# A perceiver block on one core: the first chunk's keys and values projected in the first stage, the queries last

## The chip, the core and the metric

The kernel runs on one core of a Trainium2 chip. Its engines work through their own instruction lists and wait for each other on semaphores: TensorE (PE, matmuls and transposes, with weight loads listed as PEld), VectorE (DVE), ScalarE (ACT), GpSimd (POOL), and SyncE (SP), which issues the DMAs. The metric is the device time of one execution in microseconds (us), lower is better.

## What is computed

Three layers, each added to its input: cross attention of 8 x 128 tokens over a context of 8 x 2048 rows, a differential self attention, and a mixture of eight experts. The change touches the first one alone:

```python
q = (layernorm(x) @ wq.T + bq)      # x: 8 batches x 128 tokens x 512
k = (ctx @ wk.T + bk)               # ctx: 8 batches x 2048 rows x 512
v = (ctx @ wv.T + bv)
scores = einsum('bhqd,bhkd->bhqk', q, k) / sqrt(32)    # 16 heads of 32
x = x + (softmax(scores) @ v) @ wo.T + bo
```

## The kernel before

Every product of a projection is computed as three fp32r matmuls, high x high, high x low and low x high (`product`, L41 to L45), since an operand is split in two parts: ACT copies the transposed operand out of a PSUM bank as its high part, and DVE subtracts that from the bank to get the low part. So every operand goes through a *transpose unit* on PE (four 128x128 transposes into one bank), one ACT copy and one DVE split. A *product unit* is 12 matmuls of 128x512 (four blocks of the contraction, three matmuls each) into one bank.

The program is a row of blocks with a barrier between them. The first is `queries_and_weights`. One list, `order`, is the sequence of units on PE, and the loops of ACT and DVE walk the same list: the four transpose units of wq (kind "w", 2), eight of the normalized x (kind "x"), then eight query products (kind "q", group g and half of the tokens), each followed by one transpose unit of wk or wv. Four PSUM banks are used in turn. SP loads x in two transfers, then the query bias, wq, wk, wv and the first chunk of the context; a query group is written to HBM (`q_d`) when both of its halves are out. DVE computes the layer norm of x (`Norm`: statistics, then small steps of which the square root is ACT's), writes the normalized x, and evicts the query products with their bias.

The second block is `cross_attention`. The context goes through it in 32 chunks of 512 rows, four per batch. Time is counted in beats, with eight beats for a chunk. In each beat PE's list holds at most one step of each kind: `transposed(beat)` gives the chunk and the transpose unit ("T"), every second beat; `projected(beat)` the key ("K", four) or value ("V", four) product of the chunk; from beat 20 on the scores, and from beat 32 the outputs. The loop runs from `FIRST` = -8, so that beats -8 to -1 hold the transposes of chunk 0 and beats 0 to 7 the products of chunk 0 and the transposes of chunk 1. Beat 8 begins with the first transpose unit of chunk 2. Three banks (`b_work`) are used in turn. SP loads two pieces of 256 rows per chunk into `cin`, each when its piece of the chunk before is transposed.

Output projection, self attention and the experts follow in blocks of their own, which the change does not touch.

Of the kernel before, what the change touches and what calls it, by code (L numbers as in the profile page):

```python
# [16 lines left out]
B = 8  # L17
# [48 lines left out]
class Shared:  # L66


    def __init__(self, nc, ctx):
# [18 lines left out]
        self.x_sb = at(0, "x_sb", B, D)  # L88
        self.w_sb = [at(QUARTER + i * KD * D, f"w_sb{i}", KD, D) for i in range(3)]
# [17 lines left out]
        self.q_out = [sem(f"q_out{i}") for i in range(2)]  # L107
# [10 lines left out]
class Norm:  # L118
# [20 lines left out]

    def tile_stats(self, x, t):  # L140

        self.nc.vector.bn_stats(self.stats[:, t, :], x[:, t, :]).then_inc(self.step, 1)
# [45 lines left out]
def queries_and_weights(nc, x, ctx_in, w, q_d, cin, shared):  # L188

    with ExitStack() as ctx:
# [3 lines left out]
        def sem(name):  # L197
            return ctx.enter_context(nc.semaphore(name))

        ident, x_sb, w_sb, wkT, wvT = shared.ident, shared.x_sb, shared.w_sb, shared.wkT, shared.wvT  # L200
        xn = sb("a_xn", [P, B, D])
        bq = sb("a_bq", [P, KD])
        wqT = [sb(f"a_wqT{i}", [P, KD, D], F32R) for i in range(2)]
        xT = [sb(f"a_xT{i}", [P, KD, TOK], F32R) for i in range(2)]
        q_st = sb("a_q", [P, 2, TOK])
        bank = [ctx.enter_context(nc.psum_tensor(f"a_ps{i}", [P, 512], F32)) for i in range(4)]
# [6 lines left out]
        hi_done = sem("a_hi")  # L213
        lo_done = sem("a_lo")
        normed = sem("a_normed")
        q_out = shared.q_out
# [5 lines left out]
        SPLIT = {u: i for i, u in enumerate(u for u in order if u[0] != "q")}  # L222
        RING = len(bank)
        block = ctx.enter_context(nc.Block())

        @block.sync
        def _(sp):
            for i in range(2):
                part = slice(i * (B // 2), (i + 1) * (B // 2))
                sp.dma_start(x_sb[:, part, :], x[part].rearrange("b p d -> p b d")).then_inc(x_in[i], 16)  # L230
            with nc.allow_non_contiguous_dma(reason="512 numbers"):
                sp.dma_start(bq[:, :], w["bq"].rearrange("(g p) -> p g", p=P)).then_inc(b_in, 16)
            for i in (2, 0, 1):
                sp.dma_start(w_sb[i], weights[i][0].rearrange("(o p) d -> p o d", p=P)).then_inc(w_in[i], 16)
            for c in range(2):
                sp.dma_start(cin[:, c, :, :], ctx_in[0, c * 2 * P:(c + 1) * 2 * P, :]
                             .rearrange("(o p) d -> p o d", p=P)).then_inc(shared.cin_in[c], 16)
            for g in range(G):
                sp.wait_ge(lo_done, place["q", g, 1] + 1)
                sp.dma_start(q_d[g].rearrange("b p t -> p b t"),  # L240
                             q_st[:, g % 2, :].rearrange("p (b t) -> p b t", b=B)).then_inc(q_out[g % 2], 16)
# [6 lines left out]
        def _(pe):  # L248
            pe.wait_ge(const, 2)
            for u, (kind, i, j) in enumerate(order):  # L250
                if u >= RING:
                    pe.wait_ge(lo_done, u - RING + 1)
                out = bank[u % RING]
                if kind == "w":
                    if j == 0:
                        pe.wait_ge(w_in[i], 16)
                    for o in range(KD):
                        last = nc.tensor.transpose(out[:, o * P:(o + 1) * P], w_sb[i][:, o, j * P:(j + 1) * P],
                                                   ident[:, :])
                elif kind == "x":  # L260
                    if j == 0:
                        pe.wait_ge(normed, 4 * i + 4)
                    for t in range(4):
                        last = nc.tensor.transpose(out[:, t * P:(t + 1) * P], xn[:, 4 * i + t, j * P:(j + 1) * P],
                                                   ident[:, :])
                else:
                    if (i, j) == (0, 0):

                        pe.wait_ge(lo_done, u)
                    for k in range(KD):  # L270
                        last = product(nc, out[:, :], [a[:, k, i * P:(i + 1) * P] for a in wqT],
                                       [a[:, k, j * 512:(j + 1) * 512] for a in xT], k == 0, k == KD - 1)
                last.then_inc(full, 1)

        def to(u):

            kind, i, j = u
            if kind == "w":
                return [a[:, j, :] for a in weights[i][1]]
            return [a[:, j, i * 512:(i + 1) * 512] for a in xT]  # L280

        @block.scalar
        def _(act):
            norm.scalar(act)
            for unit in SPLIT:
                act.wait_ge(full, place[unit] + 1)
                nc.scalar.activation(to(unit)[0], bank[place[unit] % RING][:, :], ACT.Copy).then_inc(hi_done, 1)

        @block.vector
        def _(dve):  # L290
            for t in range(B):
                if t % 4 == 0:
                    dve.wait_ge(x_in[t // 4], 16)
                norm.tile_stats(x_sb, t)
            norm.vector(dve)
            norm.done(dve)
            for t in range(4):
                norm.apply(x_sb[:, t, :], xn[:, t, :], t).then_inc(normed, 1)
            dve.wait_ge(b_in, 16)
# [1432 lines left out]
```

## Time and profile before

| | us |
|---|---|
| median of 3 runs | 1833.36 |
| lowest and highest | 1832.06, 1834.14 |
| the profiled execution | 1831.57 |
| its span | 1829.8 |
| PE busy in it | 1710.6 (93%) |
| DVE busy | 1200.3 (66%) |
| ACT busy | 962.1 (53%) |
| POOL busy | 695.6 (38%) |

The rows come from the profiled execution. Its span runs from the first instruction to the last; the 1.8 us beside it lie around the program. A matmul's busy time overlaps the next one's, so the distance from start to start is what a matmul or a unit costs. An idle time before a group is followed by what released it, as `<-DMA x_sb`.

### The profile page before, as it was taken

The numbers are of one execution on the slowest core, as the hardware profiler recorded it, in microseconds if no ns is written. First come the engines' busy times: TensorE is split into PE (matmuls) and PEld (weight loads), VectorE is DVE, ScalarE is ACT, GpSimd is POOL, SyncE is SP. The second block draws the span as 40 slices with busy tenths as digits, with TensorE's granted clock in tenths as the row PEclk, the third lists the DMA queues.
The fourth block names the chain that finished last, engine by engine and source line by source line (L and its number), as shares of the span: only waits on it lengthen the run. The fifth ranks groups of instructions, "written<-read, shape, count | busy, mean of one in ns | idle before, by whom it ended". The sixth has DMA issues, their size and how long they took to land. (4 is left out here: it accounts for less than half of the span.)

```text
span 1829.8 us, 37829 instructions
## 1 busy us (share of the span) xinstructions
PE 1710.6 (93%) x15768; PEld 1376.8 (75%) x15768; DVE 1200.3 (66%) x1631; ACT 962.1 (53%) x1470; POOL 695.6 (38%) x315
## 2 busy tenths in 40 slices
PE   6899999999999999999999998567999689979999
PEld 5688888888888888888888887566887466658886
DVE  5126887878778778778778787767323677753223
ACT  2236666666666666666666666653210678730000
POOL 0003555555555555555555554002001466622220
PEclk9999999999999999999999999789999899999999
DMA  4211111111011011011110101042560533101101
GB/s 162 73 47 38 32 35 41 27 39 41 27 39 42 27 39 42 28 39 37 32 39 30 39 16 63 16 132 109 179 184 2 161 91 103 58 25 46 49 19 46
DMA packets 104192, 105.00 MB, mean 57 GB/s; under 512 B 7263, under 2 KB 72799, under 8 KB 104044
## 3 DMA queue, kind: packets, MB, share of 16 engines
q1 hardware_dynamic: 104044, 102.83, 18.5%
q8 instruction: 117, 1.92, 0.4%
q14 instruction: 31, 0.25, 0.0%
HBM read 79.74 MB, written 23.07 MB: 56 GB/s over the span
## 5 line engine op out<-in xcount | busy, mean ns | idle before, releaser
L528 POOL TENSOR_TENSOR b_acc<-b_acc,b_s 128x1024 f32<-128x1024 f32 x168 | 458.6, 2730 | 268.5 <-ACT b_s L731 258.1
L793 DVE TENSOR_TENSOR b_mx<-b_psS,b_mx 128x512 f32<-128x512 f32 x480 | 331.3, 690 | 50.0 <-PE b_psS L600 36.9
L760 DVE TENSOR_TENSOR b_s<-b_s,b_mb 128x2048 f32<-128x2048 f32 x128 | 350.9, 2743 | 15.7 <-ACT b_mb L718 15.7
L731 ACT ACTIVATE b_s<-b_s 128x2048 f32<-128x2048 f32 x128 | 245.1, 1915 | 67.1 <-DVE b_s L760 67.1
L740 ACT ACTIVATE b_s<-b_psS 128x2048 f32<-128x2048 f32 x128 | 241.1, 1883 | 56.3 <-DVE b_mx L793 55.9
L43 PE MATMUL b_work<-cT,wkT 128*128 128x512 f32 x512 | 210.7, 412 | 0.0
L43 PE MATMUL b_work<-wvT,cT 128*128 128x512 f32 x512 | 209.4, 409 | 0.0
L44 PE MATMUL b_work<-cT,wkT 128*128 128x512 f32 x512 | 200.8, 392 | 0.0
L45 PE MATMUL b_work<-cT,wkT 128*128 128x512 f32 x512 | 200.5, 392 | 0.0
L45 PE MATMUL b_work<-wvT,cT 128*128 128x512 f32 x512 | 200.2, 391 | 0.0
L44 PE MATMUL b_work<-wvT,cT 128*128 128x512 f32 x512 | 200.0, 391 | 0.0
L523 POOL TENSOR_TENSOR b_acc<-b_s 128x1024 f32<-128x1024 f32 x28 | 66.9, 2389 | 281.2 <-PE b_psO L637 171.0
L690 ACT ACTIVATE b_kT<-b_work,b_bk 128x512 f32<-128x512 f32 x128 | 88.1, 688 | 157.3 <-PE b_work L45 154.8
L600 PE MATMUL b_psS<-b_q,b_kT 32*128 32x128 f32 x4096 | 152.0, 285 | 16.1 <-ACT b_s L740 16.1
L600 PEld LDWEIGHTS b_psS<-b_q,b_kT 32*128 32x128 f32 x4096 | 127.6, 188 | 41.4 <-issue 41.2
L614 PE MATMUL b_psO<-b_s,v_sb 128*32 128x128 f32 x4096 | 143.5, 282 | 6.1 <-DVE b_oq L773 4.3
L783 DVE TENSOR_TENSOR cT<-b_work,cT 128x512 fp32r<-128x512 f32 x128 | 87.4, 684 | 83.9 <-ACT cT L723 83.9
L614 PEld LDWEIGHTS b_psO<-b_s,v_sb 128*32 128x32 f32 x4096 | 108.4, 112 | 33.7 <-issue 33.2
L1679 DVE SCALAR_TENSOR_TENSOR x<-f_ps,f_gate,x 128x512 f32<-128x512 f32 x64 | 47.9, 751 | 119.7 <-PE f_ps L45 119.2
L43 PEld LDWEIGHTS b_work<-cT,wkT 128*128 128x128 f32 x512 | 96.6, 189 | 30.1 <-issue 5.6
L43 PEld LDWEIGHTS b_work<-wvT,cT 128*128 128x128 f32 x512 | 96.1, 188 | 24.5
L45 PEld LDWEIGHTS b_work<-cT,wkT 128*128 128x128 f32 x512 | 96.6, 189 | 21.4
(224 smaller groups left out, 3056.7 us busy)
## 6 DMA issues: line engine op xcount, KB each, us to landing
cin<-in_ctx SPq DMA_DIRECT2D x64, 512.0 KB, 3.7
q_scratch<-d_st SPq DMA_DIRECT2D x32, 256.0 KB, 2.5
k_scratch<-d_st SPq DMA_DIRECT2D x32, 256.0 KB, 2.5
e_q<-q_scratch SPq DMA_DIRECT2D x16, 512.0 KB, 3.5
k_sb<-k_scratch SPq DMA_DIRECT2D x64, 128.0 KB, 3.7
experts_sb<-in_L_ffn_expert_w SPq DMA_DIRECT2D x8, 1024.0 KB, 5.3
x_sb<-in_x SPq DMA_DIRECT2D x2, 1024.0 KB, 7.0
q_scratch<-a_q SPq DMA_DIRECT2D x4, 512.0 KB, 3.2
```

Of the source, the lines that this page charges most:

```text
L43: nc.tensor.matmul(out, lhs[0], rhs[0], start=first, stop=False)
L44: nc.tensor.matmul(out, lhs[0], rhs[1], start=False, stop=False)
L45: return nc.tensor.matmul(out, lhs[1], rhs[0], start=False, stop=last)
L528: nc.gpsimd.tensor_tensor(acc[:, :, :], acc[:, :, :], s[:, buf, 2 * i:2 * i + 2, :], ALU.add).then_inc(sum_done, 1)
L600: last = nc.tensor.matmul(psS[:, j, t * P:(t + 1) * P], kT[h, at + t * P:at + (t + 1) * P], q[h, m % 3, :], start=True, stop=True)
L614: last = nc.tensor.matmul(psO[j * HD:(j + 1) * HD, 0:P], v[:, at + j * HD:at + (j + 1) * HD], s[:, n % BUFS, i, j * P:(j + 1) * P], start= ...
L690: nc.scalar.activation(kT[:, at:at + 512], bank[:, :], ACT.Identity, bias=bk[:, u:u + 1]).then_inc(k_done, 1)
L731: nc.scalar.activation(part, part, ACT.Exp, scale=SCALE).then_inc(exp_done, 1)
L740: nc.scalar.activation(s[:, n % BUFS, :, :].rearrange("p t (j q) -> p t j q", j=HG), psS[:, :, :].rearrange("p j (t q) -> p t j q", t=CHUN ...
L760: nc.vector.tensor_tensor(s[:, n % BUFS, :, :], s[:, n % BUFS, :, :], mb[:, :].rearrange("p (o n) -> p o n", o=1).broadcast_to([P, CHUNK, ...
L783: nc.vector.tensor_tensor(context_place(cT[1], p, n), two(work[BANK["T", p, n]]), f32(context_place(cT[0], p, n)), ALU.subtract).then_inc( ...
L793: nc.vector.tensor_tensor(mx[:, :, :], part, mx[:, :, :], ALU.max).then_inc(mx_done, 1)
```

## The change

The first block is rewritten as `queries_and_first_chunk`. It now also transposes chunks 0 and 1 of the context and computes the four key and four value products of chunk 0. The order is: wk, chunk 0, then key and value products with the transposes of wv, chunk 1 and wq between them, then x and the queries, first half of the tokens first. It has eight banks. SP issues wk, the two pieces of chunk 0, wv, both biases, x in four transfers, wq, then the reloads of `cin`. x is placed in free columns of the key buffer `kT` and normalized there in place. ACT evicts keys, values and queries, and waits for both biases before its first instruction. The queries leave in eight transfers of 256 KB. `cross_attention` starts at beat 8: `FIRST` is 8, its counters of splits, keys and values go on from the first block's. The helpers `key_place`, `context_place` and `two` move out of `cross_attention` unchanged. The core of the diff:

```diff
-        order = ([("w", 2, k) for k in range(KD)] + [("x", half, k) for half in range(2) for k in range(KD)]
-                 + [u for n in range(2 * G) for u in (("q", n // 2, n % 2), ("w", n // KD, n % KD))])
+        order = ([("w", 0, k) for k in range(KD)] + [("c", 0, n) for n in range(4)]
...
+                 + [("x", 0, k) for k in range(KD)]
+                 + [u for g in range(G) for u in (("q", 0, g), ("x", 1, g))] + [("q", 1, g) for g in range(G)])
...
-        bank = [ctx.enter_context(nc.psum_tensor(f"a_ps{i}", [P, 512], F32)) for i in range(4)]
+        bank = [ctx.enter_context(nc.psum_tensor(f"a_ps{i}", [P, 512], F32)) for i in range(8)]
...
+            load_weights(0)
+            for h in range(2):
+                load_context(0, h)
+            load_weights(1)
             with nc.allow_non_contiguous_dma(reason="512 numbers"):
+                sp.dma_start(bk[:, :], w["bk"].rearrange("(g p) -> p g", p=P)).then_inc(b_in, 16)
                 sp.dma_start(bq[:, :], w["bq"].rearrange("(g p) -> p g", p=P)).then_inc(b_in, 16)
...
+                sp.dma_start(parts[:, g, 1:3, :], x[2 * g:2 * g + 2].rearrange("b p d -> p b d")).then_inc(x_in[g // 2], 16)
+            load_weights(2)
+            for p in range(2):
+                for h in range(2):
+                    sp.wait_ge(full, place["c", p, 2 * h + 1] + 1)
+                    load_context(p + 1, h)
...
+                elif kind == "k":
+                    if j == 0:
+                        pe.wait_ge(w_lo, counted("w", 0, KD - 1))
+                        pe.wait_ge(shared.split_done, counted("c", 0, 3))
...
+                    if j == 0:
+                        pe.wait_ge(w_lo, counted("w", 2, KD - 1))
+                        pe.wait_ge(x_lo, counted("x", i, KD - 1))
...
         @block.scalar
         def _(act):
-            norm.scalar(act)
...
+            act.wait_ge(b_in, 32)
+            for u, (kind, i, j) in enumerate(order):
+                if (kind, i, j) == ("c", 1, 2):
+                    norm.scalar(act)
+                act.wait_ge(full, u + 1)
...
+                    nc.scalar.activation(q_st[:, n % 4, :], out[:, :], ACT.Identity,
+                                         bias=bq[:, j:j + 1]).then_inc(q_done, 1)
...
+            for u, (kind, i, j) in enumerate(order):
+                if (kind, i, j) == ("w", 1, 2):
+                    statistics(0)
+                elif (kind, i, j) == ("c", 1, 0):
+                    statistics(1)
+                elif (kind, i, j) == ("c", 1, 2):
+                    norm.vector(dve)
+                    norm.done(dve)
+                elif (kind, i, j) == ("w", 2, 0):
+                    applied(0)
+                elif (kind, i, j) == ("w", 2, 2):
+                    applied(1)
...
-        FIRST, LAST = -SLOT, (SLOTS + 4) * SLOT + 3
+
+        FIRST, LAST = SLOT, (SLOTS + 4) * SLOT + 3
...
-            n = steps(beat, FIRST, 2, SLOTS * CHUNK)
+            n = steps(beat, -SLOT, 2, SLOTS * CHUNK)
...
-                if (x0 := projected(beat - 1)) is not None:
+                if beat > FIRST and (x0 := projected(beat - 1)) is not None:
```

Three places in the engines' lists follow. In them a row is line, instruction, out<-in, shape of the output and the semaphores it waits for.

SP at the start of the first block, before (x, the query bias, the weights, the context):

```order
L230 DMA x_sb<-in_x 128x4x512 x2
L232 DMA a_bq<-in_L_xattn_bq 128x4x1
L234 DMA w_sb_52<-in_L_xattn_wq 128x4x512
L234 DMA w_sb_50<-in_L_xattn_wk 128x4x512
L234 DMA w_sb_51<-in_L_xattn_wv 128x4x512
L236 DMA cin<-in_ctx 128x2x512 x2
L240 DMA q_scratch<-a_q 128x8x128 [waits a_lo] x4
```

and now (`b_kT` is where x is put):

```order
L269 DMA w_sb_49<-in_L_xattn_wk 128x4x512
L265 DMA cin<-in_ctx 128x2x512 x2
L269 DMA w_sb_50<-in_L_xattn_wv 128x4x512
L276 DMA a_bk<-in_L_xattn_bk 128x4x1
L277 DMA a_bq<-in_L_xattn_bq 128x4x1
L279 DMA b_kT<-in_x 128x2x512 x4
L269 DMA w_sb_51<-in_L_xattn_wq 128x4x512
L265 DMA cin<-in_ctx 128x2x512 [waits a_full] x4
L287 DMA q_scratch<-a_q 128x4x128 [waits a_q_done] x8
```

The bias of the queries stood behind x and now stands, with that of the keys, behind wk, two context pieces and wv; x and wq moved to the end.

ACT at the start of the first block, before (`a_full` counts the units that PE has finished):

```order
L180 ACT_TABLE_LOAD
L180 ACTIVATE a_norm_root<-a_norm_veps 128x8 [waits a_norm_step]
L287 ACTIVATE a_wqT<-a_ps 128x512 [waits a_full] x4
L287 ACTIVATE a_xT<-a_ps 128x512 [waits a_full] x8
L287 ACTIVATE wkT_63<-a_ps 128x512 [waits a_full] x4
L287 ACTIVATE wvT_65<-a_ps 128x512 [waits a_full] x4
```

and now (`a_b_in` counts the two bias transfers):

```order
L367 ACT_TABLE_LOAD [waits a_full]
L367 ACTIVATE wkT_62<-a_ps 128x512 [waits a_b_in]
L367 ACTIVATE wkT_62<-a_ps 128x512 [waits a_full] x3
L369 ACTIVATE cT_52<-a_ps 128x2x256 [waits a_full] x4
L374 ACTIVATE b_kT<-a_ps,a_bk 128x512 [waits a_full]
L367 ACTIVATE wvT_64<-a_ps 128x512 [waits a_full] x2
L374 ACTIVATE b_kT<-a_ps,a_bk 128x512 [waits a_full]
L367 ACTIVATE wvT_64<-a_ps 128x512 [waits a_full] x2
L374 ACTIVATE b_kT<-a_ps,a_bk 128x512 [waits a_full]
L369 ACTIVATE cT_52<-a_ps 128x2x256 [waits a_full] x2
```

The square root has moved behind the keys and a value unit, and a wait for the biases stands before the first copy.

PE where the last transpose unit before a query product stands, before (banks are numbered; the transpose unit is one of wk, and its bank is not read by the product behind it):

```order
L45 MATMUL a_ps0<-a_xT0,a_wqT1 128x512
L258 MATMUL a_ps1<-ident,w_sb0_50 128x128 [waits a_w_in0,a_lo]
L258 MATMUL a_ps1<-ident,w_sb0_50 128x128 x3
L43 MATMUL a_ps2<-a_xT0,a_wqT0 128x512 [waits a_lo]
L44 MATMUL a_ps2<-a_xT1,a_wqT0 128x512
```

and now, at the fifth query product (`a_x_lo` counts the splits of x):

```order
L45 MATMUL a_ps6<-a_xT0,a_wqT1 128x512
L334 MATMUL a_ps7<-ident,b_kT 128x128 [waits a_x_lo]
L334 MATMUL a_ps7<-ident,b_kT 128x128 x3
L43 MATMUL a_ps0<-a_xT0,a_wqT0 128x512 [waits a_x_lo,a_w_lo,a_q_done]
L44 MATMUL a_ps0<-a_xT1,a_wqT0 128x512
```

The product at this place now waits for the split of the unit transposed just ahead of it.

## Rows read from the trace of the kernel before

**Rows 1.** Busy by stretch: stretch, us, engines busy (instructions), PE clock, DMA, GB/s.
```profile
0.00:52.48 52.48, 34.20 (x177) 27.85 (x177) 28.99 (x58) 13.40 (x22) 0.81 (x7) 1.00 0.46 153
52.48:85.57 33.09, 28.05 (x128) 23.04 (x129) 5.35 (x8) 8.78 (x15) 0.00 (x0) 0.90 0.31 81
85.57:1200.00 1114.43, 1087.68 (x12493) 883.00 (x12495) 849.96 (x878) 714.97 (x683) 525.50 (x196) 0.99 0.13 37
```

**Rows 2.** Waits of PE, 52 to 1240 us: us in total, times, longest.
```profile
PE b_psS L600 <- ACT b_s L740: 16.1, 7, 5.0
```

**Rows 3.** Timeline of PE, context transposes of beats 2, 8: start, us, instruction.
```profile
67.81 0.60 PE L565 MATMUL b_work<-ident,cin 128*128 128x128 f32 x4
...
85.57 0.60 PE L565 MATMUL b_work<-ident,cin 128*128 128x128 f32 x4
```

**Rows 4.** Timeline of ACT, DVE and PE, 0 to 25 us.
```profile
0.73 1.28 ACT L180 ACT_TABLE_LOAD   x1 [0.73 <-PEq L1721]
6.64 2.47 DVE L142 BATCH_NORM_STATS2 a_norm_stats<-x_sb 128x6 f32<-128x512 f32 x4 [6.64 <-DMA x_sb<-in_x]
9.30 2.47 DVE L142 BATCH_NORM_STATS2 a_norm_stats<-x_sb 128x6 f32<-128x512 f32 x4 [0.19 <-DMA x_sb<-in_x]
...
12.79 0.20 DVE L159 RECIPROCAL a_norm_rstd<-a_norm_root 128x8 f32<-128x8 f32 x1 [0.27 <-ACT a_norm_root L180]
12.85 3.65 PE L258 MATMUL a_ps<-ident,w_sb 128*128 128x128 f32 x16 [12.85 <-DMA w_sb<-in_L_xattn_wq]
13.84 1.92 DVE L184 TENSOR_SCALAR a_xn<-x_sb,a_norm_mv,a_norm_rstd 128x512 f32<-128x512 f32 x4
...
19.89 4.86 DVE L315 TENSOR_TENSOR a_xT<-a_ps,a_xT 128x512 fp32r<-128x512 f32 x8
20.62 2.45 PE L264 MATMUL a_ps<-ident,a_xn 128*128 128x128 f32 x16 [1.77 <-DVE a_xT L315]
24.90 0.47 PE L43 MATMUL a_ps<-a_xT,a_wqT 128*128 128x512 f32 x1 [1.83 <-DVE a_xT L315]
```

**Rows 5.** Timeline of PE, the last unit of the first block.
```profile
50.05 0.60 PE L258 MATMUL a_ps<-ident,w_sb 128*128 128x128 f32 x4
```

**Rows 6.** Timeline of PE, start of the second block.
```profile
52.48 1.52 PE L565 MATMUL b_work<-ident,cin 128*128 128x128 f32 x12 [1.83 <-POOL b_ones L514]
...
56.92 0.66 PE L565 MATMUL b_work<-ident,cin 128*128 128x128 f32 x4 [2.92 <-DVE cT L783]
...
60.43 0.78 PE L43 MATMUL b_work<-cT,wkT 128*128 128x512 f32 x1
```

**Rows 7.** Timeline of PE, ACT and DVE, one round of query product and weight transposes.
```profile
27.74 0.60 PE L258 MATMUL a_ps<-ident,w_sb 128*128 128x128 f32 x4
...
28.38 0.60 ACT L287 ACTIVATE wkT<-a_ps 128x512 fp32r<-128x512 f32 x1 [4.67 <-PE a_ps L258]
...
29.01 0.69 DVE L315 TENSOR_TENSOR wkT<-a_ps,wkT 128x512 fp32r<-128x512 f32 x1 [0.32 <-ACT wkT L287]
...
30.93 0.60 PE L258 MATMUL a_ps<-ident,w_sb 128*128 128x128 f32 x4
```

**Rows 8.** Timeline of SP, the issue of the query bias: start, us of issue.
```profile
1.78 0.51 SPq L232 DMA_DIRECT2D a_bq<-in_L_xattn_bq  x1
```

**Rows 9.** DMA issues, 0 to 130 us: KB each, median us from issue to landing.
```profile
a_bq<-in_L_xattn_bq SPq DMA_DIRECT2D x1, 2.0 KB, 8.2
b_bk<-in_L_xattn_bk SPq DMA_DIRECT2D x1, 2.0 KB, 2.3
```

**Rows 10.** Busy by stretch, two single microseconds: columns as in the first group.
```profile
57.00:58.00 1.00, 0.58 (x4) 0.34 (x4) 1.00 (x2) 0.44 (x2) 0.00 (x0) 0.74 0.83 161
64.00:65.00 1.00, 1.00 (x5) 0.85 (x4) 0.00 (x0) 0.00 (x0) 0.00 (x0) 0.85 0.00 0
```

**Rows 11.** Timeline of ACT, the evictions of key products 0 and 1.
```profile
65.27 0.69 ACT L690 ACTIVATE b_kT<-b_work,b_bk 128x512 f32<-128x512 f32 x1 [3.85 <-PE b_work L45]
68.01 0.69 ACT L690 ACTIVATE b_kT<-b_work,b_bk 128x512 f32<-128x512 f32 x1 [2.06 <-PE b_work L45]
```

More of the change, by code:

```diff
@@ L251, in _ @@
                 if u >= RING:
-                    pe.wait_ge(lo_done, u - RING + 1)
+                    wait_evicted(*order[u - RING])
                 out = bank[u % RING]
@@ L259, in _ @@
                                                    ident[:, :])
+                elif kind == "c":
+                    h, kk = divmod(j, 2)
+                    if kk == 0:
+                        pe.wait_ge(cin_in[h], 16 * (i + 1))
+                    for k in range(2):
+                        for o in range(2):
+                            last = nc.tensor.transpose(out[:, (2 * k + o) * P:(2 * k + o + 1) * P],
+                                                       cin[:, h, o, (2 * kk + k) * P:(2 * kk + k + 1) * P], ident[:, :])
                 elif kind == "x":
@@ L270, in _ @@
                     for k in range(KD):
-                        last = product(nc, out[:, :], [a[:, k, i * P:(i + 1) * P] for a in wqT],
-                                       [a[:, k, j * 512:(j + 1) * 512] for a in xT], k == 0, k == KD - 1)
+                        last = product(nc, out[:, :], [a[:, k, j * P:(j + 1) * P] for a in wqT],
+                                       [a[:, k, i * 512:(i + 1) * 512] for a in xT], k == 0, k == KD - 1)
                 last.then_inc(full, 1)
[L275 to L280, printed above, removed]
@@ L289, in _ @@
         @block.vector
         def _(dve):
[L291 to L299, printed above, removed]
-            for u, unit in enumerate(order):
-                kind, g, half = unit
-                if u == KD:
-                    for t in range(4, B):
-                        norm.apply(x_sb[:, t, :], xn[:, t, :], t).then_inc(normed, 1)
-                if kind == "q":
-                    dve.wait_ge(full, u + 1)
-                    if g >= 2:
-                        dve.wait_ge(q_out[g % 2], 16)
-                    nc.vector.tensor_scalar(q_st[:, g % 2, half * 512:(half + 1) * 512], bank[u % RING][:, :],
-                                            bq[:, g:g + 1], None, ALU.add).then_inc(lo_done, 1)
-                else:
-                    hi, lo = to(unit)
-                    dve.wait_ge(hi_done, SPLIT[unit] + 1)
-                    nc.vector.tensor_tensor(lo, bank[u % RING][:, :], f32(hi), ALU.subtract).then_inc(lo_done, 1)
@@ L318, in cross_attention, with statistics, applied @@
-def cross_attention(nc, x, ctx_in, w, q_d, o_d, cin, shared):
+            def statistics(half):
+                dve.wait_ge(x_in[half], 32)
+                for t in range(4 * half, 4 * half + 4):
+                    norm.stats_of(xs[t], t)
+            def applied(half):
+                for t in range(4 * half, 4 * half + 4):
+                    norm.apply(xs[t], xs[t], t).then_inc(normed, 1)
+            for u, (kind, i, j) in enumerate(order):
[10 more added lines that the diff above has]
+                    applied(1)
+                count = counted(kind, i, j)
+                out = bank[u % RING]
+                if kind == "w":
+                    hi, lo = [a[:, j, :] for a in weights[i][1]]
+                    dve.wait_ge(w_hi, count)
+                    nc.vector.tensor_tensor(lo, out[:, :], f32(hi), ALU.subtract).then_inc(w_lo, 1)
+                elif kind == "c":
+                    hi, lo = [context_place(a, i, j) for a in cT]
+                    dve.wait_ge(shared.hi_done, count)
+                    nc.vector.tensor_tensor(lo, two(out), f32(hi), ALU.subtract).then_inc(shared.split_done, 1)
+                elif kind == "x":
+                    hi, lo = [a[:, j, i * 512:(i + 1) * 512] for a in xT]
+                    dve.wait_ge(x_hi, count)
+                    nc.vector.tensor_tensor(lo, out[:, :], f32(hi), ALU.subtract).then_inc(x_lo, 1)
```

132 lines of the change are left out of this document (88 added, 44 removed), and 3 rows, old and new, of the table order.

## The prediction

> **What bounds the kernel now.** I read the engines' busy times by stretch first. From 85.57 us to 1200 TensorE (PE) is busy 1087.7 of 1114.4 us and no other engine comes near it; from 0 to 52.48 it is busy only 34.2 us, and the next 33.1 us hold 5 us of idling and a granted clock of 0.90 [rows 1]. PE's waits between 52 and 1240 us come next: the largest group there is 16.1 us in seven pieces [rows 2]. So the long middle is a PE conveyor: what enters it earlier should leave it earlier, and the question is the head alone. The mark I use is beat 8 of cross attention, the transposes of chunk 2, which PE starts at 85.57 [rows 3]. From there both kernels run the same list, so the change is worth 85.57 minus the time at which PE reaches that point.
>
> The timeline of the head shows where PE idles: until 12.85 for the queries' weights, then behind norm, transposes and splits until 24.90 [rows 4]. Eight query products and eight weight transposes follow without a gap, to 50.65 [rows 5]. Then the seam between the stages to 52.48, the first chunk's transposes, their splits, and the first key product at 60.43 [rows 6].
>
> **Unit costs.** A transpose unit (four transposes) plus a 12-matmul product takes 30.93 - 27.74 = 3.19 us [rows 7]. A transpose unit plus two products is a third of 85.57 - 67.81 = 17.76, so 5.92 [rows 3]. Hence a product is 2.73 and a transpose unit 0.46 us at full clock.
>
> **What costs nothing.** All units are still done once: 16 products (4 key, 4 value, 8 query) and 28 transpose units before beat 8. The query eviction goes from VectorE (DVE) to ScalarE (ACT), x is normalized in place, x comes in four transfers instead of two, and the queries leave in eight instead of four. ACT then has about 27 us of evictions (28 of 0.6, 16 of 0.6 to 0.7 [rows 7, 11]) beside over 50 us of PE work. The context's reload for chunk 1 stands on SP's queue behind x and the queries' weights: by the pace of term 1 it lands near 24, and PE wants it near 31; if it came later than that, its lateness would be paid. Behind the seam ACT waits again for biases, some 3 us, but PE has then one transpose unit and two products (5.9 us) for the three banks.
>
> **Term 1: when the first key product can start.** It needs eight splits, four of wk and four of context chunk 0. Not PE's transposes end last there but the new first wait of ACT: it stands before every eviction and asks for both bias vectors, which SP issues behind wk, two context pieces and wv, that is behind 3 MB. Before, the two MB of x land at 6.64 and 9.30, 2.66 per MB [rows 4], and the 2 KB bias issued at 1.78 lands 8.2 later, at 9.98 [rows 8, 9]: it went behind the 2 MB and took 0.7 itself. So wv lands at 12.0 and the two biases at 13.4. The eight transpose units (four of them took 3.65 at the start [rows 4]) are done by 12 to 13.5 and fill the eight banks. From 13.4: 0.63 from ACT's first eviction to DVE's first split [rows 7], eight splits in 4.86, 0.15 until PE starts [rows 4]. Key product 0 starts at **19.0**. Bounds: 17.6 if the biases cost nothing of their own, 20.4 if each costs double.
>
> The rows show a bias that waits for what was issued before it. The Trainium skill's page "DMA: Bandwidth & Descriptors", section "Queues, rings and completion order", says that descriptors are taken in ring order, but that completion is not first-in-first-out for the issuing engine. With the first half the term is 19.0, as by the rows; if the second half let these small transfers finish well ahead, it would be that of rival A. The trace agrees with the first half (9.98 behind 9.30) and shows no case of the second.
>
> **Term 2: PE's work from there to the seam.** 16 products are 43.7 us. Eight of the 28 transpose units are done; 20 are left, 9.2 us.
>
> **Term 3: the clock.** PE has then idled for some 6 us. In the trace its granted clock falls to half at about 57.5, after a wait of 2.9 us, 0.7 of work and idling again, and is back at about 64.2 [rows 6, 10]. The key product begun in that state at 60.43 is evicted at 65.27, 4.84 later; the next eviction follows after 2.74 [rows 6, 11]. At full clock it would have been 2.73 + 0.21, so the state costs 1.9. The kernel before pays it after its seam; the changed one pays the same **1.9** at its first key product. Bounds 0 and 4.
>
> **Term 4: two stalls.** The queries' first product follows directly on its four x transpose units: before, the first such unit started at 20.62 and the product at 24.90, 4.28 [rows 4]; less 4 x 0.46 that is **2.4**. And x's last transpose unit stands right before the product that needs it: from start at 27.74 to split done at 29.01 + 0.69, plus 0.15, is 2.11 [rows 7]; less 0.46, plus 0.25 because ACT first evicts a query unit, is **1.9**. Each can be 0.5 off either way. The first has a cover: the norm's root on ACT stands behind value unit 0, evicted near 38.1, and a table load of 1.28 and a root of 0.2 follow; DVE then needs 1.05 for the small steps, 3.84 for eight tiles and 3.65 for six splits [rows 4], to 48.2. It is wanted at 49.7, so 1.5 us are in hand.
>
> **Term 5: the seam.** Before: the last transpose unit starts at 50.05 [rows 5], its split is over 1.96 later [rows 7], at 52.01, and PE starts at 52.48 [rows 6]. After: last product, eviction 0.7, issue of its query transfer 0.5 (the issue in [rows 8]), then 0.47: **1.7**.
>
> **The sum.** 19.0 + 43.7 + 9.2 + 1.9 + 2.4 + 1.9 + 1.7 = 79.8 for beat 8, against 85.57: 5.8 us earlier. The profiled execution took 1831.57 us (its span is 1829.8), so it becomes 1825.8; the three runs have their median at 1833.36, 1.8 higher, and I give the number against that: 1833.36 - 5.8 = **1827.6**. The bounds of the single terms put it between 1825 and 1830.
>
> **Rivals.**
> A. *The biases do not hold ACT.* If they land before the context (behind the seam, on an idle queue, one lands 2.3 us after its issue [rows 9]), ACT starts behind the first transpose unit and a table load, at 8.9; the splits end at 14.4, key product 0 starts at 14.5, and PE has hardly idled, so its clock stays up: 4.5 + 1.9 more, 1821.2. For: their size. Against: the 8.2 us. Chance 0.16.
> B. *Slower: the clock stays at half.* The 1.9 of term 3 came of some four fifths of a product at half clock, so a whole one costs 2.4 more. If the clock came back only after all eight key and value products, that is 19.2 instead of 1.9, and the time is 1845. It is a loss from about 3.2 products at half clock. Against: the same matmuls brought it back within 4 us [rows 6, 10]. Chance 0.05.
> C. *The biases land last.* If the 4-byte packets are served only when all 6.3 MB are in, near 22, key product 0 starts at 27.6 and the time is 1836.2; break-even is a landing at 19.2. Against: the same 8.2 us. Chance 0.06.
> D. *Given back later.* Something behind beat 8 that is tied to time and not to PE's order, such as the clock around the idle pieces near 1200, takes the gain: about 1833. Nothing in the rows ties it so. Chance 0.07.
>
> **How the numbers follow.** The forecast keeps 0.66. About 0.2%, or 3.7 us, is what a measurement of this kernel can tell from no change, so the line lies at 1829.7; of the forecast's 0.66 some 0.06 lie above it. Faster: 0.60 + 0.16 = 0.76. Within: 0.06 + 0.06 (C) + 0.07 (D) = 0.19. Slower: 0.05 (B). The range takes in the forecast's own bounds and rival A, 1820 to 1831; B, C and D are left out.
>
> **What would show it.** ACT's first eviction at about 13.4, released by a bias transfer, and PE idle before key product 0 at 19.0 (A: 14.5; C: 27.6); a granted clock of half for its first 4 us; key and value products then without gaps; a stall of 2.4 before the first query product and of 1.9 before the fifth; chunk 2's transposes at 79.8; from there to the end 1829.8 - 85.57 = 1744.2 as before (D: more). The main step is wrong if ACT's first eviction is not near 13.4, and the premise if that distance changes by more than 2 us.

## The result, and the profile after

| | before | after |
|---|---|---|
| median of 16 runs | 1834.33 us | 1828.93 us |
| lowest and highest | 1829.56, 1839.71 | 1825.63, 1831.22 |
| span of the profiled execution | 1829.8 | 1826.5 |

The ratio is 0.9972, with a 95% interval of 0.9963 to 0.9981: faster by 0.28%, or 5.4 us where 5.8 were forecast, and inside the range of 1820 to 1831. Beat 8 of cross attention, the mark of the prediction, begins at 79.98 us where 79.8 was forecast and 85.57 stood before [rows 3].

Busy time by stretch, after (stretch, us, busy and instructions of PE, PEld, DVE, ACT, POOL, granted clock, DMA share, GB/s), to be read beside [rows 1]; the cuts are beat 8 and the first instruction of the output projection:

```profile
0.00:79.98 79.98, 62.22 (x304) 52.04 (x305) 27.60 (x58) 27.23 (x47) 0.81 (x7) 0.94 0.39 128
79.98:1216.25 1136.27, 1102.37 (x12865) 896.25 (x12865) 863.99 (x888) 725.37 (x689) 525.60 (x196) 0.99 0.13 37
1216.25:1826.50 610.25, 549.86 (x2585) 432.82 (x2600) 300.94 (x677) 215.15 (x743) 168.76 (x112) 0.95 0.28 87
```

The head is 5.6 us shorter with the same PE work before beat 8. The same three stretches of before, cut at the same points of the program, were 85.57, 1136.30 and 607.93 us: the middle kept its length to 0.03 us, and the last third is 2.3 longer. So the profiled execution shows 3.3 of the 5.6 at its end, and the medians show 5.4. What became of the 2.3 is a question of its own, below.

The timeline of SP, PE, ACT and DVE at the start of the changed kernel (start, us, instruction, idle before and what ended it) answers to [rows 4] and [rows 8]:

```profile
2.30 0.77 SPq L269 DMA_DIRECT2D w_sb<-in_L_xattn_wv  x1
3.11 0.65 SPq L276 DMA_DIRECT2D a_bk<-in_L_xattn_bk  x1
3.81 1.72 SPq L277 DMA_DIRECT2D a_bq<-in_L_xattn_bq  x1
...
6.43 3.64 PE L320 MATMUL a_ps<-ident,w_sb 128*128 128x128 f32 x16 [6.43 <-DMA w_sb<-in_L_xattn_wk]
7.60 1.28 ACT L367 ACT_TABLE_LOAD   x1 [7.60 <-PE a_ps L320]
...
9.87 2.42 PE L328 MATMUL a_ps<-ident,cin 128*128 128x128 f32 x16
...
12.58 2.06 ACT L367 ACTIVATE wkT<-a_ps 128x512 fp32r<-128x512 f32 x4 [3.69 <-DMA a_bq<-in_L_xattn_bq]
13.21 2.48 DVE L414 TENSOR_TENSOR wkT<-a_ps,wkT 128x512 fp32r<-128x512 f32 x4 [13.21 <-ACT wkT L367]
...
18.23 0.77 PE L43 MATMUL a_ps<-cT,wkT 128*128 128x512 f32 x1 [5.94 <-DVE cT L418]
```

Every transpose unit that the key products need is over at 12.3. ACT sat idle for 3.69 us until the query bias landed, though the weights it was to copy began to fill the banks at 6.43. PE then idles 5.94 us until the splits are done. Landings, from issue (KB, median us), answer to [rows 9]:

```profile
w_sb<-in_L_xattn_wv SPq DMA_DIRECT2D x1, 1024.0 KB, 9.5
a_bk<-in_L_xattn_bk SPq DMA_DIRECT2D x1, 2.0 KB, 8.8
a_bq<-in_L_xattn_bq SPq DMA_DIRECT2D x1, 2.0 KB, 8.7
```

Added to the issue times: wv lands at 11.8, the key bias at 11.9, the query bias at 12.5.

The two stalls and the seam, timeline of PE, after; the first row is the first half's four x transpose units, behind value product 3:

```profile
46.90 1.91 PE L334 MATMUL a_ps<-ident,b_kT 128*128 128x128 f32 x16
...
50.85 0.47 PE L43 MATMUL a_ps<-a_xT,a_wqT 128*128 128x512 f32 x1 [2.04 <-DVE a_xT L422]
...
55.25 0.61 PE L334 MATMUL a_ps<-ident,b_kT 128*128 128x128 f32 x4
...
67.15 0.47 PE L43 MATMUL a_ps<-a_xT,a_wqT 128*128 128x512 f32 x1 [1.65 <-DVE a_xT L422]
...
79.98 0.65 PE L665 MATMUL b_work<-ident,cin 128*128 128x128 f32 x4 [1.70 <-POOL b_ones L614]
```

And the clock, single microseconds of the changed kernel (columns as above, the granted clock third from the end), as in [rows 10]:

```profile
18.00:19.00 1.00, 0.77 (x2) 0.71 (x3) 0.08 (x1) 0.00 (x0) 0.00 (x0) 0.50 1.04 383
21.00:22.00 1.00, 1.00 (x6) 0.83 (x5) 0.00 (x0) 0.00 (x0) 0.00 (x0) 0.93 1.06 389
...
52.00:53.00 1.00, 1.00 (x4) 0.82 (x3) 0.00 (x0) 0.00 (x0) 0.00 (x0) 0.50 0.08 16
55.00:56.00 1.00, 1.00 (x8) 0.76 (x7) 0.00 (x0) 0.54 (x1) 0.00 (x0) 0.87 0.00 0
```

Half clock stands at 18 us, where the prediction put it. It stands a second time from 52 to 55, behind the stall of 2.04 us, and that was not foreseen: the first query product takes 55.25 - 50.85 = 4.40 until the next unit starts. At full clock it took 2.84 in the kernel before (27.74 - 24.90 [rows 4, 7]).

**The ledger.** PE's idle pieces before beat 8 were, before, 12.85, 1.77 and 1.83 [rows 4], 1.83 and 2.92 [rows 6], and this one, in the timeline of the kernel before:

```profile
59.69 1.09 PE L565 MATMUL b_work<-ident,cin 128*128 128x128 f32 x4 [2.11 <-DMA cin<-in_ctx]
```

That is 23.3 us. After they are 6.43, 5.94, 2.04, 1.65 and 1.70: 17.8. The difference is 5.5. Besides, with four banks each four x transpose units took 2.45 us [rows 4], with eight they take 1.91, about 1.1 in all; and half clock cost some 2.2 before beat 8 in the kernel before and 2.9 in the changed one. Together that is 5.9, against 5.6 at the mark; the 0.3 between them is not explained. PE's busy time before the mark is the same in both profiles, 62.26 and 62.22 us, so the idle pieces carry the gain. The change takes 6.4 off the first wait, since wk is first in the queue where wq stood behind x's 2 MB and the bias, and 5.0 (2.92 and 2.11) off what followed the seam; it gives 5.9 back behind the bias wait.

### The profile page after: what moved, and what is told of

The parts are those of the page before. It is cut to its first block and busy times, and to the rows that moved or that the text cites. A ratio compares the mean times of both kernels' runs of the same rounds, so it can differ in the third digit from the quotient of the medians.

```text
span 1826.5 us, 37824 instructions
## 1 busy us (share of the span) xinstructions
PE 1714.4 (94%) x15753; PEld 1381.1 (76%) x15768; DVE 1192.5 (65%) x1623; ACT 967.7 (53%) x1479; POOL 695.2 (38%) x315
## 3 DMA queue, kind: packets, MB, share of 16 engines
HBM read 79.74 MB, written 23.07 MB: 56 GB/s over the span
## 5 line engine op out<-in xcount | busy, mean ns | idle before, releaser
L43 PE MATMUL b_work<-cT,wkT 128*128 128x512 f32 x496 | 203.5, 410 | 0.0
L43 PE MATMUL b_work<-wvT,cT 128*128 128x512 f32 x496 | 203.0, 409 | 0.0
L45 PE MATMUL b_work<-wvT,cT 128*128 128x512 f32 x496 | 193.9, 391 | 0.0
L44 PE MATMUL b_work<-cT,wkT 128*128 128x512 f32 x496 | 193.8, 391 | 0.0
L44 PE MATMUL b_work<-wvT,cT 128*128 128x512 f32 x496 | 193.8, 391 | 0.0
L45 PE MATMUL b_work<-cT,wkT 128*128 128x512 f32 x496 | 193.6, 390 | 0.0
L875 DVE TENSOR_TENSOR cT<-b_work,cT 128x512 fp32r<-128x512 f32 x120 | 82.0, 684 | 68.7 <-ACT cT L815 68.7
L43 PEld LDWEIGHTS b_work<-cT,wkT 128*128 128x128 f32 x496 | 93.0, 187 | 29.4 <-issue 5.6
L45 PEld LDWEIGHTS b_work<-cT,wkT 128*128 128x128 f32 x496 | 93.1, 188 | 20.6
```

The costliest lines, as they stand in the source:

```text
L43: nc.tensor.matmul(out, lhs[0], rhs[0], start=first, stop=False)
L44: nc.tensor.matmul(out, lhs[0], rhs[1], start=False, stop=False)
L45: return nc.tensor.matmul(out, lhs[1], rhs[0], start=False, stop=last)
L875: nc.vector.tensor_tensor(context_place(cT[1], p, n), two(work[BANK["T", p, n]]), f32(context_place(cT[0], p, n)), ALU.subtract).then_inc( ...
```

## The experiments

All times of beat 8 are those of the first transpose unit of chunk 2 on PE, in the profiled execution of each kernel; ratios are against the kernel before, from runs on the same chip.

### A later bias wait

The wait moves to the first eviction that uses a bias.

```diff
-            act.wait_ge(b_in, 32)
             for u, (kind, i, j) in enumerate(order):
+                if (kind, i, j) == ("k", 0, 0):
+                    act.wait_ge(b_in, 32)
```

> One edit to the changed kernel: ACT's wait for both biases moves from before its first instruction to before the eviction of key product 0, the first that uses one. Theory (the bias wait alone sets the start of the key products, and the idling it causes costs PE its clock): ACT's first eviction at 8.9 instead of 12.58, behind the table load; the last split is then bound by PE's last transpose unit, key product 0 starts at 13.9 instead of 18.23 and runs at full clock, 2.73 instead of 4.17; chunk 2's transposes start 5.7 us earlier, at 74.2, and the time falls by about 5.7 against the changed kernel, near 0.994 of the kernel before. Rival (something else ends just behind the bias wait, such as the context, wv or x by DMA): key product 0 or a unit within the next 20 us waits for a DMA, and less than 3 us are gained.

Timeline of ACT and PE of this kernel:

```profile
7.43 0.60 ACT L368 ACTIVATE wkT<-a_ps 128x512 fp32r<-128x512 f32 x1 [5.42 <-PE a_ps L320]
...
13.59 0.47 PE L43 MATMUL a_ps<-cT,wkT 128*128 128x512 f32 x1 [2.28 <-DVE cT L419]
...
72.47 0.65 PE L666 MATMUL b_work<-ident,cin 128*128 128x128 f32 x4 [1.71 <-POOL b_ones L615]
```

The first key product starts at 13.59 instead of 18.23, and beat 8 comes at 72.47, 7.5 earlier than in the changed kernel. Of these, 4.6 are the start and 1.3 the clock at the first product (2.82 until the next unit instead of 4.17); the remaining 1.6 are the second half-clock phase, which is missing here although the stall before the first query product is as long as before. That part is not the edit's: the phase is missing in a second execution of the unchanged program too, below. The time is 1822.3 us, ratio 0.9939 (0.9918 to 0.9959), which puts it some 6 us below the changed kernel. ACT started even earlier than expected, because its table load now runs at 0.73 and no longer behind PE's first unit. The rival is out: no unit of the next 20 us waited for a DMA. So the wait's place cost the changed kernel 4.6 us of start and at least 1.3 of clock, and that is shown.

### Biases last in the queue

Both bias loads move behind `load_weights(2)`, the wait stays at ACT's head.

> One edit to the changed kernel: SP issues the two biases behind x and the queries' weights instead of ahead of x; ACT's wait stays at its head. Theory: the landing follows the 3 MB now ahead of them, 7.9 us later by the pace of 2.65 us per MB, so ACT's first eviction goes from 12.58 to 20.5, key product 0 from 18.23 to 26.1, and the end by the same 7.9: the time is about 1837, 1.001 to 1.002 of the kernel before, and all of it passes through the long middle. Rival (the middle or the tail takes up a shift of the head): chunk 2's transposes start 7.9 later, but the time grows by less than 5.

```profile
20.99 2.06 ACT L367 ACTIVATE wkT<-a_ps 128x512 fp32r<-128x512 f32 x4 [12.15 <-DMA a_bq<-in_L_xattn_bq]
...
26.64 0.77 PE L43 MATMUL a_ps<-cT,wkT 128*128 128x512 f32 x1 [14.82 <-DVE cT L418]
...
59.67 0.47 PE L43 MATMUL a_ps<-a_xT,a_wqT 128*128 128x512 f32 x1 [2.04 <-DVE a_xT L422]
...
63.66 1.06 PE L334 MATMUL a_ps<-ident,b_kT 128*128 128x128 f32 x4
...
88.81 0.65 PE L665 MATMUL b_work<-ident,cin 128*128 128x128 f32 x4 [1.70 <-POOL b_ones L614]
```

3 MB more ahead of the biases made them 8.4 us later, where 7.9 was expected: from the landing of wv at 12.1 to that of wq at 20.5 the 3 MB took 2.8 us each. The key bias landed at 20.3 and the query bias at 21.0, so the first came 0.3 ahead of wq, which was issued before it. Beat 8 is 8.8 later than in the changed kernel, at 88.81. The time is 1837.6 us, the ratio 1.0013 (1.0001 to 1.0025). By the ratios that is 7.5 us above the changed kernel, with an uncertainty of some 3; the medians, 1837.6 and 1828.9, were not taken side by side. This is the course of rival C, brought about by the order of issue, and the rival of this run, that less than 5 us would arrive at the end, is unlikely. The second half-clock phase is there, behind a stall of 2.04 us again: the first query product takes 63.66 - 59.67 = 3.99.

### Four bias loads instead of two

Each bias is loaded a second time into a tile that nothing reads, and ACT waits for all four.

```diff
+                sp.dma_start(bk2[:, :], w["bk"].rearrange("(g p) -> p g", p=P)).then_inc(b_in, 16)
+                sp.dma_start(bq2[:, :], w["bq"].rearrange("(g p) -> p g", p=P)).then_inc(b_in, 16)
...
-            act.wait_ge(b_in, 32)
+            act.wait_ge(b_in, 64)
```

> One edit to the changed kernel: each bias is loaded twice, the second time into a tile that nothing reads, and ACT waits for all four. It measures what one 2 KB bias transfer in that queue costs. Theory (about 0.7 each, in queue order): ACT's first eviction at 14.0 instead of 12.58, key product 0 at 19.6. Rival (they go beside the large transfers and the cost is that of the 3 MB): 12.6 and 18.2 again.

```profile
12.87 2.06 ACT L371 ACTIVATE wkT<-a_ps 128x512 fp32r<-128x512 f32 x4 [3.98 <-DMA a_bq<-in_L_xattn_bq]
...
18.52 0.77 PE L43 MATMUL a_ps<-cT,wkT 128*128 128x512 f32 x1 [6.38 <-DVE cT L422]
```

The timeline of SP in this kernel, and the landing of wq, which the queue holds behind the biases and x:

```profile
9.52 3.55 SPq L283 DMA_DIRECT2D b_kT<-in_x  x4
```

```profile
w_sb<-in_L_xattn_wq SPq DMA_DIRECT2D x1, 1024.0 KB, 8.7
```

ACT started 0.29 us later. The expectation of 0.7 each is refuted: it had read the distance from the second MB of x to the bias before, 0.68 us, as the bias's own cost, and that distance hardly depends on the number. From the landing of the last MB ahead to that of the last bias it was 0.7 with one bias (before), 0.7 with two (11.8 to 12.5) and 0.7 with four (12.1 to 12.8). The 0.29 is no clear price either, for wv, which is ahead of the biases, landed 0.3 later in this execution. So two more loads cost ACT at most 0.3 us, and the rival, which gave nothing, is not excluded.

What stands behind them paid more. SP issued the first transfer of x at 9.52 instead of 5.57, the queue moved 17 and 74 GB/s in the two microseconds from 11 to 13 where the changed kernel had 124 and 396, and wq, issued at 13.10, landed at 21.8 where it landed at 20.6 in the six executions with two biases at this place. Nothing waited for x or wq then, so the time doesn't show it: beat 8 stands at 80.00 and the ratio is 0.9948 (0.9931 to 0.9965), which with four runs says nothing against the changed kernel's 0.9972. Why SP's issue took longer was not tried.

### PE kept busy through the wait

The transpose unit that is last before the key products is done nine times into its bank, which ACT reaches late anyway.

```diff
+                    for _ in range(9 if (i, j) == (0, 3) else 1):
```

> One edit to the changed kernel: PE repeats the transpose unit that is last before the key products eight times more, 3.7 us of work into the same bank, so that it hardly idles while ACT waits for the biases and evicts. The extra transposes are over near 16.1, when ACT comes to that bank, so the splits end as before, and key product 0 starts at 18.2 to 18.6. Theory (the idling costs the clock): no half clock at 18 to 22, key product 0 takes 2.73 instead of 4.17, chunk 2's transposes 1.4 earlier than 79.98, and 1.7 more if the second fall is missing too. Rival (the clock is low there for another reason): still 4.2 for key product 0.

```profile
9.92 5.50 PE L329 MATMUL a_ps<-ident,cin 128*128 128x128 f32 x48
18.24 0.47 PE L43 MATMUL a_ps<-cT,wkT 128*128 128x512 f32 x1 [2.83 <-DVE cT L419]
21.09 1.04 PE L320 MATMUL a_ps<-ident,w_sb 128*128 128x128 f32 x8
...
77.10 0.65 PE L666 MATMUL b_work<-ident,cin 128*128 128x128 f32 x4 [1.71 <-POOL b_ones L615]
```

The first key product starts at the same time as in the changed kernel and takes 2.85 until the next unit, instead of 4.17: the idling of 5.9 us had cost 1.3. The profiles of the changed kernel and its variants agree: behind 5.9 us of idling or more the first key product took 4.17, 4.60, 5.26, 5.26 and 5.26, and behind 2.83 or less 2.82 to 2.85, in three of them. Beat 8 comes 2.9 earlier, the second phase being missing too. The time is 1827.3, ratio 0.9959 (0.9946 to 0.9972); against the changed kernel's 0.9972 the intervals overlap, and the changed kernel run again on the same chip has 1827.9. So the gain is shown in the trace only.

### The x transposes moved ahead

```diff
-                    ("v", 0, 1), ("w", 2, 0), ("w", 2, 1), ("v", 0, 2), ("w", 2, 2), ("w", 2, 3), ("v", 0, 3)]
-                 + [("x", 0, k) for k in range(KD)]
-                 + [u for g in range(G) for u in (("q", 0, g), ("x", 1, g))] + [("q", 1, g) for g in range(G)])
+                    ("v", 0, 1), ("w", 2, 0), ("w", 2, 1), ("v", 0, 2), ("w", 2, 2), ("w", 2, 3)]
+                 + [("x", 0, k) for k in range(KD)] + [("v", 0, 3)]
+                 + [("q", 0, 0), ("x", 1, 0), ("x", 1, 1), ("q", 0, 1), ("x", 1, 2), ("q", 0, 2), ("x", 1, 3), ("q", 0, 3)]
+                 + [("q", 1, g) for g in range(G)])
...
-                elif (kind, i, j) == ("w", 2, 2):
+                elif (kind, i, j) == ("x", 1, 0):
                     applied(1)
```

> Two moves in the changed kernel's list: the first half's four x transpose units go ahead of value product 3 (and the second half's normalization behind them), and the last x transpose unit of the second half goes one product ahead, so that no product stands right behind the units it waits for. ACT's bias wait stays. Theory: both stalls before query products (2.0 and 1.7) go, and with the first of them the second fall of the clock (1.7), so chunk 2's transposes start at 74.6 instead of 79.98 and the time falls by some 5. Rival (the clock falls for another reason than the stall): only 3.7 are gained and the granted clock still shows half near 52 us.

```profile
18.13 0.77 PE L43 MATMUL a_ps<-cT,wkT 128*128 128x512 f32 x1 [6.02 <-DVE cT L419]
23.39 1.45 PE L321 MATMUL a_ps<-ident,w_sb 128*128 128x128 f32 x8
...
45.56 1.91 PE L335 MATMUL a_ps<-ident,b_kT 128*128 128x128 f32 x16
...
75.61 0.65 PE L666 MATMUL b_work<-ident,cin 128*128 128x128 f32 x4 [1.71 <-POOL b_ones L615]
```

PE no longer waits for x anywhere, and there is no second half-clock phase. Beat 8 comes at 75.61, 4.4 earlier. The first phase lasted longer in this execution: the first key product takes 23.39 - 18.13 = 5.26. The changed kernel's second execution, below, had the same 5.26 and no second phase either, and against its 79.74 the gain is 4.1, of which the two stalls are 3.7. That the phase goes with the stall is therefore not shown: of six executions that kept the stall of 2.04 us two had half clock behind it and four had not. The time is 1826.1, ratio 0.9939 (0.9918 to 0.9961).

### All three edits together

> The later bias wait and both moves of the x units together. Theory: the two gains add: 5.7 and 5.4, chunk 2's transposes at 68.9, the time about 11 below the changed kernel, 0.991 of the kernel before. Rival (with an earlier start of the products something queued by time becomes late, first the context's reload for chunk 1 and the queries' weights, which land near 22.4 at the earliest): PE shows a wait for a DMA between 20 and 35 us and the sum falls short by its length.

```profile
14.36 0.47 PE L43 MATMUL a_ps<-cT,wkT 128*128 128x512 f32 x1 [1.82 <-DVE cT L420]
...
69.00 0.65 PE L667 MATMUL b_work<-ident,cin 128*128 128x128 f32 x4 [1.71 <-POOL b_ones L616]
```

Beat 8 stands at 69.00 where 68.9 was expected. Some luck is in that: 1.7 of the expected 5.4 are the second phase, of which it is not shown that the edit removes it, and the first key product starts 0.8 later than with the later bias wait alone (14.36 against 13.59), since the eight transpose units ahead of it ran longer in this execution (from 6.51 to 12.54, against 6.31 to 11.32). The time is 1814.0 us, ratio 0.9892 (0.9867 to 0.9917): 21.6 us below the kernel before on the same chip, of which the head explains 16.6. The interval, from four runs, is 15.2 to 24.4 us, so the rest need not mean anything. No DMA is waited for between 20 and 35 us. This version beats both kernels.

### The old seam, shortened in the kernel before

The second stage's biases are loaded in the first stage, and SP loads the first queries only behind the context reloads.

```diff
-            for i in range(2):
-                sp.wait_ge(shared.q_out[i], 16 * (G // 2))
...
             for beat in range(FIRST, LAST):
+                if beat == 0:
+                    for i in range(2):
+                        sp.wait_ge(shared.q_out[i], 16 * (G // 2))
+                    for n in range(3):
+                        load_queries(n)
```

> The kernel before with its seam shortened and nothing else: the second stage's two biases are loaded in the first stage, and SP waits for the queries' write-out and loads the first queries at beat 0, behind the context reloads for chunk 1. It tells how much of the change's 5.6 us was the old seam's. Theory: ACT's first copy behind the seam starts at 53.1 instead of 55.48, the last split of chunk 0 ends near 56.5, the reload for chunk 1 lands near 57.2 instead of 59.7, and key product 0 starts at 57.6 instead of 60.43; with the clock kept up 1.9 more: chunk 2's transposes at 80.9 to 82.7 instead of 85.57, the time 3 to 4.6 below the kernel before. Rival (the seam was not what the change saved, its gain is in the first 50 us): less than 1 us.

```profile
55.03 0.66 PE L567 MATMUL b_work<-ident,cin 128*128 128x128 f32 x4 [0.67 <-DVE cT L785]
57.89 0.63 PE L567 MATMUL b_work<-ident,cin 128*128 128x128 f32 x4 [2.20 <-DMA cin<-in_ctx]
...
83.18 0.60 PE L567 MATMUL b_work<-ident,cin 128*128 128x128 f32 x4
```

The split's wait shrinks from 2.92 to 0.67 us [rows 6], the wait for the context's reload stays, 2.20, and the matmuls behind it still run at half clock until 62. Beat 8 comes 2.4 earlier than before, at 83.18; the time is 1833.1 against 1835.5, ratio 0.9991 (0.9981 to 1.0001), which is not told from no change. So at the mark this part of the old seam is worth less than half of the change's 5.6, and less than the theory said, since the reload binds right behind it. The rival's "less than 1 us" misses the mark as well; the time decides nothing, for its interval runs from 3.5 us gained to 0.2 lost.

### The changed kernel once more

> The changed kernel once more, with no edit, to see what two executions of one program share. In six profiles the distance from chunk 2's transposes to the end was 1739.9 to 1750.7 us, without order by the length of the head. Theory (the half-clock phases near the end of cross attention and behind it fall otherwise in every execution): the head comes out as before, chunk 2's transposes at 79.98 within 0.5 but for the second clock fall, which may be missing; the distance to the end differs from 1746.5 by 1 us or more, and with it the total at half clock. Rival (that distance belongs to the kernel): 1746.5 within 0.5 again.

```profile
18.16 0.77 PE L43 MATMUL a_ps<-cT,wkT 128*128 128x512 f32 x1 [6.08 <-DVE cT L418]
23.42 1.33 PE L320 MATMUL a_ps<-ident,w_sb 128*128 128x128 f32 x8
...
52.16 0.47 PE L43 MATMUL a_ps<-a_xT,a_wqT 128*128 128x512 f32 x1 [2.04 <-DVE a_xT L422]
55.00 0.60 PE L334 MATMUL a_ps<-ident,b_kT 128*128 128x128 f32 x4
...
79.74 0.65 PE L665 MATMUL b_work<-ident,cin 128*128 128x128 f32 x4 [1.71 <-POOL b_ones L614]
```

The same program, and the start of the first key product and the stalls are the same, but the clock is not: that product took 5.26 instead of 4.17, and the second phase is missing, 2.84 behind a stall of 2.04 again. The time is 1827.9, ratio 0.9965 (0.9952 to 0.9978), which agrees with the first comparison. The distance to the end, 1746.6, equals the first execution's 1746.5, against the expectation; its two parts do not. The last 90 us of cross attention by stretch, the first execution and then this one:

```profile
1126.25:1216.25 90.00, 56.10 (x1386) 49.06 (x1385) 67.91 (x72) 51.29 (x32) 0.00 (x0) 0.83 0.21 63
```

```profile
1129.20:1219.20 90.00, 56.42 (x1310) 49.41 (x1301) 65.70 (x68) 48.91 (x30) 0.00 (x0) 0.77 0.20 62
1219.20:1826.30 607.10, 545.59 (x2585) 429.59 (x2600) 300.92 (x677) 214.75 (x743) 169.35 (x112) 0.96 0.29 87
```

A granted clock of 0.77 instead of 0.83 goes with 1139.5 instead of 1136.3 us from beat 8 to the output projection, and 0.96 instead of 0.95 behind it with 607.1 instead of 610.3. The others agree: over these last 90 us the granted clock was 0.83 in the kernel before and in the one with all three edits (first parts of 1136.3 and 1137.3), 0.81 with the old seam short, and 0.77 in the five others (1139.0 to 1140.1). For ten profiled executions (us; the parts are beat 8 to output projection, and from there to the end):

| kernel | beat 8 | first part | second part | median of runs |
|---|---|---|---|---|
| before | 85.57 | 1136.3 | 607.9 | 1834.3 |
| changed | 79.98 | 1136.3 | 610.3 | 1828.9 |
| changed, again | 79.74 | 1139.5 | 607.1 | 1827.9 |
| four bias loads | 80.00 | 1139.5 | 608.3 | 1826.6 |
| PE kept busy | 77.10 | 1139.0 | 606.8 | 1827.3 |
| x ahead | 75.61 | 1140.1 | 610.6 | 1826.1 |
| later bias wait | 72.47 | 1139.1 | 606.4 | 1822.3 |
| all three | 69.00 | 1137.3 | 602.7 | 1814.0 |
| old seam short | 83.18 | 1139.8 | 604.2 | 1833.1 |
| biases last | 88.81 | 1140.0 | 604.7 | 1837.6 |

The parts scatter by 4 and 8 us without order by the head's length, while median less beat 8 stays within 4 us of its mean, and is 1748.8 before and 1749.0 in the changed kernel. The 2.3 us that the changed kernel's profile lost behind 1216 are therefore scatter of one execution, not a price of the change. The kernels did not all run on one chip: the later bias wait, the biases last, x ahead and all three ran on one, the other four experiments on another. Part of the scatter may be the chip's, but the first four differ among themselves by 2.8 in the first part and by 8 in the second. Why the second part was shortest in the version with all three edits was not tried; its profiled execution was the fastest of its four runs.

## Why the prediction was right, and where it was not

**Premise.** That the middle is PE's and hands on what the head saves held: 1136.30 against 1136.27 us in the two profiles compared first, and a shift of 8.8 at beat 8 in the other direction gave 7.5 by the ratios, within their uncertainty of 3. The sign given for it, 1744.2 within 2 us to the end, was missed by 0.3 (1746.5): it was too tight for two single executions, as the table shows (1739.9 to 1750.7).

**Term 1, 19.0 forecast, 18.23 measured.** The mechanism was right: ACT's bias wait ends last (3.69 us on it), it follows the 3 MB ahead of it, and the version without it starts at 13.59. The term that was mis-sized is the biases' own 0.7 each: the two together landed 0.7 behind wv, and two more made at most 0.3. That is 0.7 of the 0.8 too much; wv, at 11.8 instead of 12.0, is the other part. The 5.6 from ACT's first eviction to the first key product came out to 0.01 (18.23 - 12.58). The Trainium skill's page "DMA: Bandwidth & Descriptors", section "Queues, rings and completion order", has descriptors taken in ring order and completion in no fixed order; the traces agree with the first (11.8, 11.9, 12.5, in issue order; 8.4 later with 3 MB more ahead) and show the second once, by 0.3 us (the key bias at 20.3, wq at 20.5, with the biases last); no bias landed well ahead of the MB before it.

**Term 2, 52.9.** Nothing in it failed. Against the measured rows some 0.6 us are missing in the whole sum. A product right behind a transpose unit took 2.81 to 2.87 until the next start where 2.73 was counted, a dozen times, and a transpose unit took 0.40 in a pair and 0.35 to 0.37 alone where 0.46 was counted, which gives a good part back.

**Term 3, 1.9 forecast, 1.3 measured,** and 2.4 in the second execution. The cause is shown by the run that kept PE busy. What was wrong was to count one such phase: behind the stall before the queries came a second one in the first execution, 1.6 us, and none in the second. Term 4 had priced that stall as idle time alone.

**Term 4, 2.4 and 1.9 forecast, 2.04 and 1.65 measured.** Both stood where they were put, and moving the x units removed both. The cover of the first held: DVE had done all that stands ahead of x's first split and idled 1.47 us for ACT's copy there.

**Term 5, 1.7 forecast, 1.70 measured.**

**The sum.** 79.8 against 79.98 is closer than its parts, and that is luck: 0.8 too much in the first, 0.6 in the third and 0.6 in the fourth term, against 1.6 for the phase not foreseen and 0.6 in the second. The range of "between 1825 and 1830" is narrower than the terms' own bounds: added up they give 1823 to 1832.

**The rivals.** A did not happen, but its price was sound: without the bias wait at its head the first key product starts at 13.6 (14.5 in A) and the time is 1822.3 (1821.2 in A). C's course was built: the first key product at 26.6 and 1837.6, against the 27.6 and 1836.2 given. B did not happen: in every profile the clock was back to full some 3 to 6 us behind the start of the first key product. D's sign, a longer way from beat 8 to the end, stood in both profiles of the changed kernel (1746.5 and 1746.6 against 1744.2), but that distance scatters by 10 us without order. D falls by the medians: 5.4 of the 5.6 arrive, and at least 3.5 by the interval.

## What to carry to other kernels

An engine's first wait holds everything behind it: put a wait for a small operand at the instruction that reads it, for its landing is that of the queue before it (here 12.5 us for 2 KB, and 4.6 us of start). To issue the operand ahead of the megabytes is the other way; no run here tried it, and the run with four bias loads is a warning that what stands behind them can come later. When a head is shortened, list PE's idle pieces before and after; their difference (23.3 less 17.8) was nearly the whole gain, and a piece can bring a product at half clock besides: those of 6 us or more did each time, those of 2 us in some executions. Read a gain of a few microseconds at the landmark where the kernels join and from medians, not from the ends of two single profiles.

## What the runs showed of the hardware that was not expected

- One program's half-clock phases differ from execution to execution: the first key product took 4.17 and 5.26 us, a stall of 2.04 us was followed by half clock in one execution and by full clock in the next (in two of six over all kernels that had it), and the same last 90 us of cross attention had a granted clock of 0.83 and 0.77. The Trainium skill's page "TensorE: Matmul & The Clock Gate", Part 1, says that the number of slow matmuls at a start varies from run to run of one kernel; the trace agrees (1.3 and 2.4 us lost).
- The last of the 2 KB bias loads landed some 0.7 us behind the MB ahead of it, whether there were one, two or four (0.4 where they stood behind wq). With four, SP issued x at 9.52 instead of 5.57, and wq behind it landed at 21.8 instead of 20.6. When the biases stood behind wq, the first of them landed 0.3 us before it.
- A table load on ACT ran at 0.73 us in the two variants of the changed kernel without the bias wait at the head of ACT's list, and at 7.56 to 7.71, behind PE's first unit, in the six executions with it.
